# Six of sixteen drives of a selective scan made by TensorE instead of VectorE, and the side work of that layer sent through one PSUM bank

## What is computed

```python
u = silu(conv(x @ in_w.T) + conv_b);  z = the other half of x @ in_w.T
x_dbl = u @ xproj_w.T                 # dt (8), B (16), C (16) for each token
delta = softplus(dt @ dt_w.T + dt_b)
dA  = exp(delta * A)                  # "decay", per token, channel, state
dBu = delta * B * u                   # "drive", per token, channel, state
h = dA * h + dBu                      # the scan over tokens, per state
y = sum over states of C * h, + u * Dp
out = (y * silu(z)) @ out_w.T
```

## Time and profile before

| | |
|---|---|
| three runs | 4429.82, 4434.05 (median), 4446.77 us |
| profiled execution | 4444.85 us, span 4443.0 us |
| mean granted TensorE clock | 0.844 |
| busy share of the span | PE 77%, DVE 63%, ACT 39%, POOL 22% |
| the scan layer's units | from about 2495 to 3587 us of the span |

### The profile page before, as it was taken

The page is one execution under the profiler, slowest core; times in us unless marked ns, Lnnn a source line. Parts: engine busy times, 40 slices in busy tenths (PEclk is TensorE's granted clock), DMA queues, the critical chain, the costliest instruction groups (busy, mean ns, idle before and its releaser), DMA issues. The chain is left out here.

```text
span 4443.0 us, 45602 instructions
## 1 busy us (share of the span) xinstructions
PE 3420.7 (77%) x12125; PEld 1525.2 (34%) x12125; DVE 2788.2 (63%) x4212; ACT 1718.9 (39%) x2599; POOL 976.4 (22%) x516
## 2 busy tenths in 40 slices
PE   5498997799996489877799576766767668767998
PEld 2122224444443144434444222222222234533443
DVE  6867762433345566635433799999999963355444
ACT  2045564244434134443333444545455413312222
POOL 3100000000002100000000476777777720100000
PEclk7569897799998578887899788888888878878999
DMA  4411111000003522210000333333333310000000
GB/s 132 103 34 52 50 40 31 0 0 0 0 24 109 128 60 72 70 49 0 0 0 0 116 124 116 132 116 122 124 124 124 124 55 0 2 0 0 0 0 19
DMA packets 127676, 250.63 MB, mean 56 GB/s; under 512 B 22245, under 2 KB 97658, under 8 KB 110202
## 3 DMA queue, kind: packets, MB, share of 16 engines
q1 hardware_dynamic: 126506, 247.34, 17.0%
q0 software_dynamic: 1024, 1.58, 0.2%
HBM read 191.98 MB, written 56.89 MB: 56 GB/s over the span
## 5 line engine op out<-in xcount | busy, mean ns | idle before, releaser
L1814 POOL TENSOR_TENSOR a_g<-a_g,a_spread 128x1024 f32<-128x1024 f32 x256 | 659.9, 2584 | 576.6 <-DVE a_g L1772 576.6
L1574 PE MATMUL a_y<-a_g,ident 128*128 128x512 f32 x768 | 458.2, 736 | 359.7 <-POOL a_g L1819 216.0
L883 DVE TENSOR_REDUCE a_top<-a_sc 128x1 f32<-128x512 f32 (+3 forms) x1024 | 568.0, 589 | 264.9 <-PE a_sc L772 143.3
L848 ACT ACTIVATE a_prob<-a_st 128x1024 f32<-128x1024 f32 (+2 forms) x512 | 439.2, 865 | 476.1 <-PE a_st L789 294.6
L1772 DVE TENSOR_TENSOR_SCAN a_g<-a_decay,a_drive 128x512 f32<-128x512 f32 x512 | 596.5, 1206 | 0.0
L455 DVE TENSOR_TENSOR f_s<-f_a,f_spread 128x512 f32<-128x512 f32 x392 | 267.9, 687 | 434.8 <-ACT f_a L440 268.8
L769 PE MATMUL a_sc<-a_k,a_q 72*128 72x512 bf16 (+3 forms) x1024 | 402.4, 404 | 138.4 <-DMA a_k<-a_k_rows 63.1
L1694 ACT ACTIVATE a_decay<-a_delta,a_capped_a 128x512 f32<-128x512 f32 x512 | 337.2, 712 | 430.6 <-DVE a_capped_a L1744 235.4
L422 PE MATMUL f_y<-f_s,f_w 128*128 128x512 f32 x784 | 401.3, 599 | 21.1 <-DVE f_s L455 20.4
L415 PE MATMUL f_hid<-h,f_w 128*128 x784 | 404.9, 601 | 6.1 <-PEq L246 6.1
L1574 PEld LDWEIGHTS a_y<-a_g,ident 128*128 128x128 f32 x768 | 163.5, 227 | 629.3 <-issue 401.0
(11 more groups left out here) (323 smaller groups left out, 4688.3 us busy)
## 6 DMA issues: line engine op xcount, KB each, us to landing
a_spread<-a_bc_rows SPq DMA_DIRECT2D x128, 1024.0 KB, 4.6
a_q<-a_q_rows SPq DMA_DIRECT2D x64, 288.0 KB
a_pv_rows<-a_pv_sb SPq DMA_DIRECT2D x64, 256.0 KB, 2.0
a_q_rows<-p_qp SPq DMA_DIRECT2D x72, 128.0 KB
a_q_rows<-a1q_qp SPq DMA_DIRECT2D x72, 128.0 KB
a_k_rows<-a1q_kp SPq DMA_DIRECT2D x72, 128.0 KB
a_k<-a_k_rows SPq DMA_DIRECT2D x32, 288.0 KB
a_k_rows<-p_kp SPq DMA_DIRECT2D x72, 64.0 KB
```

What stands on the lines that cost most here:

```text
L848: nc.scalar.activation(prob[w % 2][:, j, 0:width(kp)], st[:, j % 2, 0:width(kp)], ACT.Exp, scale=a.scale).then_inc(s.exp_done, 1)
L883: nc.vector.tensor_reduce(top[:, t, n:n + 1], sc[:, t % 2, 0:w], AX.X, ALU.max).then_inc(s.maxed, 1)
L1574: last = nc.tensor.matmul(y[:, k, :], S.ident[:, :], g[:, n % 8, k, :], start=(n == 0), stop=False)
L1814: nc.gpsimd.tensor_tensor(g[:, n % 8, :, :], g[:, n % 8, :, :], spread[:, pair % 4, 2 + n % 2:3 + n % 2, :].to_broadcast([P, H2, L]), ALU. ...
```

## The change

- `BY_PE` names six states (4, 6, 8, 10, 12, 14) whose drive PE makes. POOL makes a second copy of du in SBUF (`pool_du`), PE turns it to tokens on partitions in two parts (`pe_flip_du`), ACT copies it (`act_du`). PE turns the rows of B and C (`pe_flip_b`), ACT copies them (`act_b`), and for each of the six states ACT makes four diagonal matrices of B, 128 tokens each (`act_diag`). `pe_drive` then makes half a drive with four 128x128 products. DVE keeps 20 of 32 products a unit. `drive` has three banks instead of two, used in turn.
- `bank` is one bank instead of two. So conv, z, xproj, B, dpre, out, project and the turned du pass through it one by one, each read (by ACT, or by DVE for out) before the next is written. ACT copies conv and z out (`act_conv`, `act_z`) and applies silu later, to both halves at once.
- The slots of the side work move: conv half 1 at slot 0, du at 1, conv half 0 at 2, z at 3 and 4, silu at 4, out at 5, project at 6, xproj at 7, B and dpre half 0 at 8, dpre half 1 at 9. DVE does `gated` after state 3 and `o` after state 5.
- DVE's order inside a state is now scan, next state's drive, scan, next state's drive.

```diff
@@ -1456,6 +1456,10 @@
     UNITS = 2 * NB
     LAG = 3
     PAIRED = (1, 4, 6, 11)
+    BY_PE = (4, 6, 8, 10, 12, 14)
+    NPE, NDVE = len(BY_PE), STATES - len(BY_PE)
+    BY_DVE = [n for n in range(STATES) if n not in BY_PE]
+    DIAGS = 2
...
             gated, o = si("gated", [P, H2, L]), si("o", [P, 2, L])
-            bank = inner.enter_context(nc.psum_tensor("a2_bank", [P, 2, L], F32))
+            du_sb, du_turned = si("du_sb", [P, H2, L]), si("du_turned", [P, TC, H2, P])
+            b_turned = si("b_turned", [P, 2, TC, 2 * STATES])
+            b_diag = si("b_diag", [P, DIAGS, TC, P])
+            bank = inner.enter_context(nc.psum_tensor("a2_bank", [P, L], F32))
             y = inner.enter_context(nc.psum_tensor("a2_y", [P, H2, L], F32))
             du = inner.enter_context(nc.psum_tensor("a2_du", [P, H2, L], F32))
-            drive = inner.enter_context(nc.psum_tensor("a2_drive", [P, H2, L], F32))
+            drive = inner.enter_context(nc.psum_tensor("a2_drive", [P, 3, L], F32))
             bc_rows = nc.dram_tensor("a2_bc_rows", (2, 2 * STATES, L), F32).ap()
...
+            def slot(n, k):
+                return (2 * n + k) % 3
+            def freed(U, n, k):
+                q = 2 * n + k
+                return H2 * STATES * U + q - 2 if q >= 3 else H2 * STATES * (U - 1) + (31, 32, 30)[q]
+            def pe_drive(U, n, k):
+                i = BY_PE.index(n)
+                if k == 0:
+                    nc.tensor.wait_ge(diag_done, NPE * U + i + 1)
+                    nc.tensor.wait_ge(du_copied, 2 * U + 2)
+                nc.tensor.wait_ge(scanned, freed(U, n, k))
+                for t in range(TC):
+                    last = nc.tensor.matmul(drive[:, slot(n, k), t * P:(t + 1) * P], du_turned[:, t, k, :],
+                                            b_diag[:, i % DIAGS, t, :], start=True, stop=True)
+                last.then_inc(pe_driven, 1)
+            def pe_flip_du(U, half):
+                if half == 0:
+                    nc.tensor.wait_ge(du_sb_done, U + 1)
+                else:
+                    nc.tensor.wait_ge(du_copied, 2 * U + 1)
+                for t in range(2):
+                    for k in range(H2):
+                        at = (2 * half + t) * P
+                        last = nc.tensor.transpose(bank[:, (2 * t + k) * P:(2 * t + k + 1) * P], du_sb[:, k, at:at + P],
+                                                   S.ident[:, :])
+                last.then_inc(du_flipped, 1)
...
+            def pe_z(b, d, k):
+                nc.tensor.matmul(bank[:, :], pack[d][:, INNER + k * P:INNER + (k + 1) * P], h_of(b),
+                                 start=True, stop=True).then_inc(z_done, 1)
...
-            def pe_dpre(d, V):
-                nc.tensor.wait_ge(sz_done, 2 * V + 2)
-                nc.tensor.wait_ge(xp_copied, V + 1)
-                for k in range(H2):
-                    nc.tensor.matmul(bank[:, k, :], dt_w[d][96:, k * P:(k + 1) * P], xp[96:, :],
-                                     start=True, stop=True).then_inc(dpre_done, 1)
+            def pe_dpre(d, V, k):
+                if k == 0:
+                    nc.tensor.wait_ge(b_copied, V + 1)
+                else:
+                    nc.tensor.wait_ge(soft_read, 2 * V + 1)
+                nc.tensor.matmul(bank[:, :], dt_w[d][96:, k * P:(k + 1) * P], xp[96:, :],
+                                 start=True, stop=True).then_inc(dpre_done, 1)
...
                 U = 2 * b + d
+                V = U + 1
                 nb, nd = (b, 1) if d == 0 else (b + 1, 0)
                 for n in range(STATES):
-                    if n < TAPS and not last_unit:
-                        if n == 0:
+                    if n == 0 and not last_unit:
+                        nc.tensor.wait_ge(soft_read, 2 * U + 2)
+                        pe_conv(nb, nd, 1)
+                    if n == 1:
+                        if last_unit:
                             nc.tensor.wait_ge(soft_read, 2 * U + 2)
-                        pe_conv(nb, nd, 1, (TAPS - 1 - n,))
-                    if n >= LAG:
-                        pe_gate_sum(U, d, n - LAG)
-                    elif not first:
-                        pe_gate_sum(U - 1, 1 - d, STATES - LAG + n)
-                    if n == 4 and not first:
-                        nc.tensor.wait_ge(soft_read, 2 * U + 1)
+                        else:
+                            nc.tensor.wait_ge(conv_read, 2 * V + 1)
+                        pe_flip_du(U, 0)
+                    if n + 1 in BY_PE:
+                        pe_drive(U, n + 1, 0)
+                    pe_sum_of_slot(U, d, n, first)
+                    if n == 1:
+                        pe_flip_du(U, 1)
+                    if n + 1 in BY_PE:
+                        pe_drive(U, n + 1, 1)
+                    if n == 2 and not last_unit:
+                        nc.tensor.wait_ge(du_copied, 2 * U + 2)
+                        pe_conv(nb, nd, 0)
+                    if n == 3 and not last_unit:
+                        nc.tensor.wait_ge(conv_read, 2 * V + 2)
+                        pe_z(nb, nd, 1)
+                    if n == 4 and not last_unit:
+                        nc.tensor.wait_ge(z_read, 2 * V + 1)
+                        pe_z(nb, nd, 0)
+                    if n == 5 and not first:
+                        if last_unit:
+                            nc.tensor.wait_ge(du_copied, 2 * U + 2)
+                        else:
+                            nc.tensor.wait_ge(z_read, 2 * V + 2)
                         pe_out(U - 1, 1 - d)
-                    if n == 5 and not first and d == 0:
+                    if n == 6 and not first and d == 0:
                         pe_project(b - 1, U - 1)
                     if last_unit:
                         continue
-                    if n == 6:
-                        nc.tensor.wait_ge(soft_read, 2 * U + 1)
+                    if n == 7:
+                        nc.tensor.wait_ge(z_read, 2 * V + 2)
                         wait(nc.tensor, o_done, U)
                         wait(nc.tensor, p_done, b)
-                        pe_conv(nb, nd, 0)
-                    if n == 7:
-                        pe_z(nb, nd, U + 1)
+                        pe_xproj(nd, V)
                     if n == 8:
-                        pe_xproj(nd, U + 1)
+                        pe_flip_b(V)
+                        pe_dpre(nd, V, 0)
                     if n == 9:
-                        pe_dpre(nd, U + 1)
+                        pe_dpre(nd, V, 1)
+            def act_conv(d, V, k):
+                nc.scalar.wait_ge(conv_done, 2 * V + 2 - k)
+                nc.scalar.activation(soft_t[:, k, :], bank[:, :], ACT.Identity, bias=w(d, "conv_b")[:, k:k + 1]
+                                     ).then_inc(conv_read, 1)
+            def act_z(V, k):
+                nc.scalar.wait_ge(z_done, 2 * V + 2 - k)
+                nc.scalar.activation(soft_r[:, k, :], bank[:, :], ACT.Copy).then_inc(z_read, 1)
...
+                nc.scalar.wait_ge(conv_read, 2 * V + 2)
+                wait(nc.scalar, y_done, V - 1)
+                nc.scalar.activation(u[:, d, :, :], soft_t[:, :, :], ACT.Silu).then_inc(u_done, 1)
+                nc.scalar.wait_ge(z_read, 2 * V + 2)
+                wait(nc.scalar, gated_done, V - 1)
+                nc.scalar.activation(sz[:, d, :, :], soft_r[:, :, :], ACT.Silu).then_inc(sz_done, 1)
...
+            def act_diag(U, d, n):
+                i = BY_PE.index(n)
+                col = 4 * (n // 2) + n % 2
+                nc.scalar.wait_ge(b_copied, U + 1)
+                wait(nc.scalar, pe_driven, H2 * (NPE * U + i - DIAGS + 1))
+                for t in range(TC):
+                    last = nc.scalar.activation(b_diag[:, i % DIAGS, t, :], S.ident[:, :], ACT.Identity,
+                                                scale=b_turned[:, d, t, col:col + 1])
+                last.then_inc(diag_done, 1)
...
+                    if n == 0 and not last_unit:
+                        act_conv(nd, V, 1)
+                    if n == 1:
+                        act_du(U, 0)
+                        act_du(U, 1)
+                    if n + 3 in BY_PE:
+                        act_diag(U, d, n + 3)
+                    if n == 2 and not last_unit:
+                        act_conv(nd, V, 0)
+                    if n == 3 and not last_unit:
+                        act_z(V, 1)
+                    if n == 4 and not last_unit:
+                        act_z(V, 0)
+                        act_silu(nd, V)
                     if n == 6 and not first and d == 0:
...
                         continue
                     if n == 7:
-                        act_silu(nd, U + 1)
+                        act_copy_xproj(V)
                     if n == 8:
-                        act_copy_xproj(U + 1)
+                        act_b(nd, V)
+                        act_soft(nd, V, 0)
                     if n == 9:
-                        act_soft(nd, U + 1)
```

(38 more changed lines are left out.)

148 lines of the change are left out of this document (89 added, 59 removed).

## The result

The changed kernel takes 4592.12 us, median of 4 runs (4589.56 to 4596.24), against 4433.46 us for the kernel before (4 runs): a ratio of 1.0353, 95% interval 1.033 to 1.0376, thus 158.7 us slower. The forecast was 4535 us, in a range of 4440 to 4620: the sign and the main cause are right, the size is 57 us short.

What follows compares the result with a forecast made beforehand. DVE's order of work was taken to bound the scan layer. Per inner unit, 12.45 us of waits against 7.1 removed and 0.9 already waited gave +4.45; together +61, plus 41 for PE's clock, +102: 4535 us, range 4440 to 4620.

Steps and rivals of the forecast that it cites:

- Removed from DVE: Six of 16 states lose two DVE drives each: 7.1 us a unit, 113 us over 16 units.
- place 1: State 4, second half: PE's half drive stands behind the gate sum that waits for `gated`; DVE waits 1.45 us.
- place 2: State 5's decay: ACT reads z(1) first, so DVE waits 1.15 us.
- place 3: `o` after state 5: out stands behind state 6's half drives in PE's slot 5; DVE waits 2.95 us.
- place 4: State 6's decay: ACT does table loads and two silus first; DVE waits 0.9 us.
- place 5: States 9 and 10: decays come late behind xproj, B and dpre work; DVE waits 0.65 and 2.35 us.
- place 6: First softplus factor: ACT's queue, with four diagonals for state 12, delivers the square late; DVE waits 3.0 us.
- The clock: A fifth of 14.5 us of PE passes in places 1 to 5 at half speed: +2.9 us a unit, +41 in 14.
- Rival D: PE's queue, cut by short waits, runs half the chains' passes at 1.2 GHz: +191, about 4625 us; chance 0.14.
- The wait at the start: Two convolutions and two z take turns on one bank at the layer's start: +2 us, bounds 0 and 4.
- the one on POOL: POOL's extra product of 1024 elements, 2.6 us, fits its sum of 52 us in a unit of 74: hidden.
- Rival B: DVE stays the bound: unit 62.9 us, time 4321 us, with small waits up to 4410; chance 0.08.

Runs made afterwards that it cites:

- experiments 2: Changed kernel with out put ahead of the two half drives in PE's slot 5: 4587.13 us, ratio 1.0346.
- 3: Changed kernel with DVE's four softplus factors one state later, after states 11 to 14: 4575.63 us, ratio 1.0303.
- 4: Changed kernel with `gated` back after state 2, as in the kernel before: 4541.78 us, ratio 1.0228.
- 7: Changed kernel with ACT making each decay one slot earlier, ahead of the reads of the bank: 4579.52 us, ratio 1.0321.
- experiment 12: Kernel of experiment 11 with POOL's pair sum after state 12 dropped and the fourth factor between state 14's halves: 4401.25 us, ratio 0.9904.
- Experiments 5: Changed kernel with factors and `delta` directly behind a state's second scan, ahead of the next drive: 4574.27 us, ratio 1.0313.
- 6: Kernel of experiment 1 with factors and `delta` directly behind the scan, ahead of the next drive: 4512.69 us, ratio 1.0166.
- 8: Changed kernel with the edits of experiments 2, 3, 4, 5 and 7 together: 4457.24 us, ratio 1.0043.
- experiment 10: Kernel of experiment 8 with all drives back on DVE and nothing turned or copied for PE: 4443.43 us, ratio 1.0008.
- experiment 1: Changed kernel with all drives back on DVE, keeping the one bank, side-work order, joint silus and DVE's order by halves: 4624.02 us, ratio 1.0425.
- experiment 11: Kernel of experiment 8 with state 10 back on DVE, and `du` started together with POOL's copy: 4438.38 us, ratio 1.0006.

## Why the prediction was right, and where its size was off

**Removed from DVE: right.** 192 drives, 114.5 us by the rows, 113 by the sum.

**The seven waits inside a unit: right in place, cause and nearly in size.** Predicted against read in the timeline above and in the unit after it: place 1, 1.45 against 2.84 and 2.99; place 2, 1.15 against 1.10 and 1.09; place 3, 2.95 against 2.76 and 2.77; place 4, 0.9 against 1.14 and 0.77; place 5, 0.65 + 2.35 against 0.53 and 1.35, and 2.49 both times; place 6, 3.0 against 3.54 and 3.81. The sum is 12.45 against 14.4 and 15.3. Two of the seven are not quite as forecast. Place 1, the drive that waits for PE, was more than twice its size in the mean of the layer: 52.4 us in 15 waits. At place 4 of the first of these units the trace names PE's gate sum (`a_y`), not the decay, which had ended at 3002.80, 0.60 us before the scan started (0.22 in the next unit); six waits of that kind make 6.8 us, and no run tells what they are. That each was a wait was shown by the edit that moved it (experiments 2, 3, 4, 7); that they are not independent was not foreseen. As a forecast of the change this did no harm, since all were there; as a guide to mending it, it misled me twice (2 and 7).

**The clock: right in sum, in one place.** With its 2.9 us the forecast had 15.35 us of waits for each inner unit, and the fourteen have 14.9 in the mean. But it had spread the 2.9 over all places, so that the sum fits is luck in part. Most of it was place 1, where PE, after 2.87 us of waiting for `gated`, took its four passes of the gate sum at half speed (granted clock 0.50 from 2990 to 2992; 3.48 us, where the four behind the next half drive took 1.88):

```profile
2989.16 3.48 PE L1585 MATMUL a_y<-a_g,ident 128*128 128x512 f32 x4 [2.87 <-DVE a_gated L1904]
...
2996.93 1.88 PE L1585 MATMUL a_y<-a_g,ident 128*128 128x512 f32 x4
```

Rival D did not come: the granted clock over 2960 to 3500 is 0.86, against 0.84 over the same window before.

**The wait at the start: too small.** It was put at +2, bounds 0 and 4. The first factor of the first unit waits 33.7 us where it waited 20.4: +13. Convolutions, z, and their reads take turns on one bank, with no scans to hide them. Every variant with the one bank kept it (32.8 to 35.3), the fastest too. The term was mis-sized by 11 us.

**What the sum lacked: DVE's products against POOL's, +38 us.** The step that failed is the one on POOL: "hidden", since its sum fits in the unit. It weighed POOL's busy time only, and not what POOL's running does to DVE. Rows of the kernel before showed it already: the first factor took 2.06 and 3.17 us for a product that takes 1.2 elsewhere, and POOL's mean was 2584 ns; I took these as they were. The interleaving that the diff makes visible (`dve_drive(U, n + 1, 1)` between scan and factor) should have been asked what starts during that 0.58 us: POOL's product, released by the scan.

**The size, laid out.** By the rows the layer grew by 157 us, against 102. Inner units went from 69.0 to 78.7 us, +9.7 instead of +7.35: 33 us in fourteen. Of these, products with two SBUF inputs make +36 and the `a_peak` step -11; most of the remaining 8 is that six states given away shortened DVE's work by less than 7.1 us a unit (over fifteen units, overlaps counted once, drives took 110 us less and scans 10 more, so 6.65 a unit). The start adds 12, the first unit 5 (it waits 12.1 us, where "about 0" left room for 7.1), and the last 5 (2.0 us longer instead of 2.7 shorter). Of the profile foretold, DVE's busy share came as forecast (81% from the first `du` to the last), the unit of 74 to 77 us did not.

**Rival B** (DVE stays the bound, 4321) came nearer in experiment 12, but DVE there still waits some 2.6 us in each unit for the first factor, and 35.3 us at the start. **Left open:** whether PE's drives are worth anything in the order of experiment 12. Experiments 5 and 6, and 8 and 10, say that they are not, each in its own order; the pair to experiment 12 without them was not run. Nor was the kernel before with its own collisions taken apart (150.7 us in those 96 products, where 1.2 us each would be 115, and 14.4 in the `a_peak` step, where 2.7 are enough: some 47 us, more than the 34 by which experiment 12 beats it in the medians), so of the 0.96% the part that belongs to this change is not known.

## What to carry to other kernels

Taking work off the bounding engine pays only if its other inputs come from queues that do not wait for that engine in turn: here 113 us were removed and 235 us of waits came back. The bank alone does not make them (in experiment 10 it costs nothing inside the units), nor do the drives alone: it is one chain of side work through PE, ACT and the bank, in which DVE's next input stands behind work that waits for DVE. When a diff puts one short instruction between two others, ask which other engine the first one releases, and whether it then starts ahead of the second. Waits on one chain are not costs of their own: mending one moves much of it to the next (38.5 us taken at one place, 30.6 back at another; 83 taken, 86 back), so judge an edit by the time, and the place with all its neighbours mended.

## What the runs showed of the hardware

A DVE product with two SBUF inputs (128x1024, f32) takes 1.20 us if it starts before POOL's, which then takes 3.25 instead of 2.35. If POOL's started first, DVE's ends 1.1 us after POOL's end, so that it takes 1.2 to 3.4 us in all, by how much of POOL's was left. Over all fourteen traces of the layer, 449 such products started 0.03 to 0.23 us ahead of POOL's and took 1.19 to 1.23 us; 642 started 0.08 to 3.17 us behind POOL's start and ended 1.08 to 1.20 us after its end, without an exception. Started within 0.05 us of each other, as `du` and its copy in experiment 11, DVE kept its 1.23 us and POOL's took 3.40. In the whole layer the order alone was worth 111 us (experiment 1 against 6).

Not only products of two tiles: the TENSOR_SCALAR on `a_peak`, two elements a partition and one tile as input, took 0.94 to 0.95 us and ended 0.02 to 0.03 us after POOL's product in all 60 cases in which it started under one (traces of the kernel before and of experiments 5, 6 and 12), and 0.17 us otherwise. The reduction that writes `a_peak` right before it, also with one input, kept its 1.22 us in every run.
